# Moving half of the attention output projection out of the last head into a stage of its own

## The reference

```python
kqv = layernorm(x) @ Wqkv + bqkv                 # k, q, v in this order
scores = einsum('bsnh,btnh->bnst', k, q) / sqrt(128)   # masked, softmax
x = x + attn_out @ Wo + bo                       # Wo is 2048 x 2048
g = layernorm(x) @ Wg.T;  u = layernorm(x) @ Wu.T      # dequantized from uint8
x = x + (silu(g) * u) @ Wd.T                     # 8192 inner columns
```

## Time and profile before

| | us |
|---|---|
| median of 3 runs | 3152.21 |
| the profiled execution | 3151.75 |
| its span, first to last instruction, slowest core | 3150.1 |
| spans of the eight cores | 3135.9 to 3150.1 |
| TensorE matmul busy in the span | 2486.1 |
| VectorE busy | 990.5 |
| ScalarE busy | 789.9 |

### The profile page before, as it was taken

How to read it: one execution, slowest core, us unless ns; L and a number is a source line. 1 busy time by engine, 2 the same in 40 slices (tenths; PEclk the granted TensorE clock), 3 DMA queues, 4 the chain that set the end, 5 groups by cost and what they waited for, 6 DMA issues and landing times.

```text
span 3150.1 us, 31073 instructions; the slowest of 8 cores (3135.9 to 3150.1 us)
## 1 busy us (share of the span) xinstructions
PE 2486.1 (79%) x12388; PEld 1158.7 (37%) x12624; DVE 990.5 (31%) x1236; ACT 789.9 (25%) x1076; POOL 26.2 (1%) x49
## 2 busy tenths in 40 slices
PE   1256777777777777745554799999999999999998
PEld 0123333334433333311222344444444444444443
DVE  0354333333333333312334323222222223232322
ACT  0233333333333333300100230303131221313030
POOL 0000000000000000000000000000000000000000
PEclk9977999999999999955577899999999999999999
DMA  7744111111111111030033110101010111101012
GB/s 98 145 144 108 21 21 21 21 21 31 31 21 21 21 21 21 1 120 27 14 102 106 56 51 21 51 21 51 20 51 31 44 37 39 43 31 51 20 41 107
DMA packets 26573, 149.46 MB, mean 47 GB/s; under 512 B 2400, under 2 KB 2448, under 8 KB 19008
## 3 DMA queue, kind: packets, MB, share of 16 engines
q0 software_dynamic: 6848, 55.19, 8.8%
q1 hardware_dynamic: 18720, 86.51, 8.2%
q10 hardware_dynamic: 864, 5.77, 0.5%
HBM read 173.15 MB, written 16.78 MB: 60 GB/s over the span
## 4 chain that ended last, share of the span: by engine, by line
PE 69%; DVE 12%; ACT 7%; issue 6%; DMA 3%; another core or an unknown queue 2%; DVEq 0%; ACTq 0%; POOL 0%; POOLq 0%; SPq 0%
PE PB L183 35%; PE PJP L183 16%; PE SC L183 12%; DVE STAT L183 6%; PE TP L183 3%; PE OP L183 3%; DVE YS L183 3%; ACT VF L183 1%; ACT PT L183 1%; ACT PS L183 1%; ACT PTB L183 1%; DVE PS L183 1%; DVE SC L183 1%; DMA YS<-x_q 1%
## 5 line engine op out<-in xcount | busy, mean ns | idle before, releaser
L183 PE MATMUL PJP<-XHF,WQKVB 128*128 128x512 bf16 x1967 | 481.1, 394 | 25.5 <-ACT KS L183 15.8
L183 PE MATMUL PB<-YF,GD 128*128 128x512 bf16 x2008 | 454.6, 382 | 23.1 <-DVE YS L183 18.3
L183 PE MATMUL PB<-YF,UD 128*128 128x512 bf16 x2007 | 450.0, 379 | 2.2
L183 PEld LDWEIGHTS PJP<-XHF,WQKVB 128*128 128x128 bf16 x2048 | 206.1, 101 | 278.9 <-issue 70.3
L183 PEld LDWEIGHTS PB<-YF,GD 128*128 128x128 bf16 x2048 | 200.9, 98 | 267.7 <-issue 30.5
L183 DVE SCALAR_TENSOR_TENSOR HBUF<-PB,USC,SIG 128x1024 bf16<-128x1024 f32 x64 | 82.2, 1284 | 681.9 <-PE PB L183 681.9
L183 PEld LDWEIGHTS PB<-YF,UD 128*128 128x128 bf16 x2048 | 200.4, 98 | 241.6
L183 ACT ACTIVATE SIG<-PB,GSC 128x1024 f32<-128x1024 f32 x64 | 71.3, 1114 | 739.4 <-PE PB L183 739.4
L183 PE MATMUL SC<-DDG,HBUF 128*128 128x512 bf16 x1003 | 224.6, 379 | 13.7 <-DVE HBUF L183 12.6
L183 PE MATMUL PB<-DDG,HBUF 128*128 128x512 bf16 x1003 | 224.8, 379 | 1.1
L183 PE MATMUL PJP<-WOC,OS 128*128 128x512 bf16 x249 | 115.0, 611 | 102.4 <-DVE YS L183 88.1
(11 more groups left out here) (71 smaller groups left out, 1724.5 us busy)
## 6 DMA issues: line engine op xcount, KB each, us to landing
GUD<-u_blob SPq DMA_DIRECT2D x62, 768.0 KB, 4.3
WQKVB<-f_blob POOLq DMA_DIRECT2D x16, 1536.0 KB, 12.4
XT<-x_full SPq DMA_DIRECT2D x16, 1024.0 KB, 6.1
WOC<-wo_bf SPq DMA_DIRECT2D x12, 1024.0 KB, 6.1
wo_bf<-f_blob POOLq DMA_DIRECT2D x1, 8192.0 KB, 97.3
XT<-x_q SPq DMA_DIRECT2D x8, 1024.0 KB, 5.9
WOC<-wo_bf POOLq DMA_DIRECT2D x8, 1024.0 KB, 6.0
out<-YS POOLq DMA_DIRECT2D x8, 1024.0 KB, 4.2
```

The costliest lines, as they stand in the source:

```text
L183: r = getattr(e, meth)(*args, **kw)
```

## The change

The 64 projection groups in the last head go, and with them the waits that stood for them. The output projection stage now takes all 16 contraction chunks c = 0 to 15 in each of its 8 bursts, so each WOC buffer is filled twice per burst. The first load of WOC0 now waits for the last product of the head (attn_last), as that of WOC1 does already. The 8 loads of x into YS are all issued by POOL, each behind the one before; they are emitted after the head in the program, but POOL has nothing between. At the end the stores of odd row tiles are issued by ScalarE and not by POOL.

```diff
-            if h == HEADS - 1:
-                for _ in range(8):
-                    if tw_state["idx"] < len(tail_groups):
-                        emit_tail_wo()
             emit_tav()
...
+    ev_xq = []
+    p.wait("gpsimd", xhf_rel)
...
+    for j in range(QT):
+        if j:
+            p.wait("gpsimd", ev_xq[-1])
+        ev_xq.append(p.op("gpsimd", "dma_start",
+                          out=YS[:, j * 2048:(j + 1) * 2048],
+                          in_=xq_hbm[j * 128:(j + 1) * 128, :], inc="sxq",
+                          dma=True))
...
-    woc_rel = [[tw_state["last_mm"]], [attn_last]]
+    woc_rel = [[attn_last], [attn_last]]
...
-            for c in range(8, NCH):
+            for c in range(NCH):
...
-                            start=(c == 8), stop=last_c,
+                            start=(c == 0), stop=last_c,
...
-                p.wait("vector", [ev_wo_j[jl], ev_xq[j]]
-                       + tail_ev.get((j, dh), []))
+                p.wait("vector", [ev_wo_j[jl], ev_xq[j]])
...
-    ev_out = None
+    ev_out = [None, None]
     for j in range(QT):
-        p.wait("gpsimd", final_evac[j])
...
+        qeng = "gpsimd" if j % 2 == 0 else "scalar"
+        p.wait(qeng, final_evac[j])
...
+                             inc=SO if j % 2 == 0 else "so2", dma=True)
```

More of the change, by code:

```diff
@@ L593, in build_nc @@
     tp_rel_tp = tp_rel
[L594 to L634, removed]
     for h in range(HEADS):
@@ L758, in build_nc @@
                 p.wait("tensor", ev_woc)
-                if c == 8:
+                if c == 0:
                     p.wait("tensor", [os_done, pj_rel[0], pj_rel[1]])
@@ L932, in build_nc @@
             hbuf_rel[cc2] = ev_dn_last
-    ev_out = None
+    ev_out = [None, None]
     for j in range(QT):
-        p.wait("gpsimd", final_evac[j])
[L937 to L940, removed]
+        qeng = "gpsimd" if j % 2 == 0 else "scalar"
+        p.wait(qeng, final_evac[j])
+        ev_out[j % 2] = p.op(qeng, "dma_start",
+                             out=out_hbm[j * 128:(j + 1) * 128, :],
+                             in_=YS[:, j * 2048:(j + 1) * 2048],
+                             inc=SO if j % 2 == 0 else "so2", dma=True)
+    p.wait("gpsimd", ev_out[0])
+    p.wait("gpsimd", ev_out[1])
     p.build()
```

## The result

| | before | after |
|---|---|---|
| median of 10 runs each, us | 3152.75 | 3060.38 |
| the same without the runs with a lowered clock, us | 3151.35 | 3057.08 |
| ratio, 95% interval | | 0.9702 [0.969, 0.9714] |
| the profiled execution, us | 3151.75 | 3056.95 |
| its span, us (spans of the eight cores) | 3150.1 | 3055.4 (3045.5 to 3055.4) |

Forecast were 3057 us and a range of 3033 to 3092. In some executions, of either kernel, the cores of one half of the chip are granted a lower clock and take some per cent longer; such runs raise the first row of the table and are left out of every ratio and of every median that follows. The second row is 94.3 us apart, and the ratio gives 93.9.

A forecast was written before the change was run, and what follows sets the result against it. The last head's 64 small projection groups were taken as a chain of TensorE-VectorE round trips. Head, first burst, seven bursts and rest: 62.4 + 30.0 + 140.0 + 103.3 = 335.7 for 429.6; with stores -0.5, 3057 us, range 3033 to 3092.

The forecast's parts named there:

- The head: Last attention head, first score matmul to last copy: only its own chain stays, 62.4 us for 250.0, bounds 58 to 67.
- What is gained: Last head and projection stage: same number of matmuls, the gain is 64 small round trips between TensorE and VectorE.
- The loads of x: Eight chained loads on POOL during the last head: 54 us, hidden; nothing taken, 6 us kept for the range.
- The first burst: Start of the projection stage, no chunk loaded: ends 30.0 us after the head, 12.9 more, bounds 25 and 36.
- The seven bursts: Later projection bursts of 64 matmuls with load waits: 20.0 us each, 140.0 in place of 59.2.
- The rest of the stage: Projection stage outside the bursts, VectorE's adding, bias and layer norm with TensorE waiting: 103.3 us, unchanged.
- The stores: Final stores, odd row tiles issued by ScalarE: -0.5 us, between -1 and +1.
- The sum: Last head plus projection stage: 335.7 us for 429.6, -93.9; with the stores 3057 us in all.
- Loads in a crowd: Rival, projection bursts: eight cores' loads take 8.0 us instead of 6.0, +16, 3073 us; chance 0.12.
- Cold bursts: Rival, projection bursts: waits inside keep the clock at half, 27.7 us per burst, 3119 us; chance 0.10.
- Warm bursts: Rival, projection bursts: more matmuls make the cold start vanish, 17.5 us per burst, 3038 us; chance 0.05.
- Slower: Rival, projection stage: chunk loads become the bound, slower than before from 17.8 us landing, 3169 us at 20; chance 0.03.

The follow-up runs named there:

- four buffers: The changed kernel with two more Wo buffers, filled beside the last head, so that a burst has all four chunks; ratio 0.9577, median 3016.99 us.
- late weight loads: The changed kernel with ScalarE's two 768 KB GUD loads issued behind the first pair of row tiles, not at the head's end; ratio 0.9692, median 3050.97 us.

## Why the prediction was right, point by point

- **The head.** 62.4 us forecast, 62.36 measured (six cores 62.4, two 60.9). The chain of the attention alone could be read from the pieces between the groups. That it fits to a tenth is chance; the bounds were 58 and 67. The head is a chain of short operations on three engines: TensorE is busy for 28.1 of the 62.4 us, at a clock of 0.56.
- **What is gained.** The prediction closes its sum with "what is gained is the 64 small round trips". That is half of it. The number of matmuls is the same, but TensorE's busy time in head and stage falls from 226.0 us (140.09 + 85.88) to 181.2 (28.11 + 19.27 + 133.83): 44.8 of the 89.6 us that the traces show are the same matmuls taking less time, for the most part at a faster clock. The sum had this inside its measured terms (8.46 us for 32 matmuls in a burst, 14.9 for 32 in the small groups), without saying so.
- **The loads of x.** 54 us and hidden, forecast. They are issued from 1338.40 to 1377.95, one every 5.6 us and not 6.8, 45 us in all, and the last is in before the head ends. The stall of 24.4 us that went with them was worth 17 to 20 by itself.
- **The first burst.** 30.0 forecast, 36.3 measured, just outside the bounds of 25 and 36; the other seven cores have 33.2 to 35.5. This is the term that was mis-sized. "I take 11 for WOC0, near the middle" was one step: with four loads in flight the first matmul came 13.6 us after the head; without the GUD loads it came after 7.2. That is 2.6 of the 6.3 us. The other 3.7 are in "8.5 + 7.0 + 3.5": from the first matmul on 22.7 us passed and not 19.0 (18.4 to 22.7 on the eight cores, median 20.4), at a clock of 0.74. The first 32 matmuls took 9.61 us and not 8.46, and from their end 13.1 us passed and not 10.5, the last 32 taking 9.91 behind a wait of 3.43. The 8.46 were those of bursts that TensorE enters after some 5 us of standing. The runs show that this matters, though not in a strict order: 32 matmuls took 7.07 us after 0.52 us of idle time and 8.64 after 8.42 (four buffers), 9.44 after 7.6 (late weight loads) and 9.61 after 14.
- **The seven bursts.** 140.0 forecast, 137.65 measured, 19.66 each (130.5 to 138.2 on the eight cores). The windows of the longest and the shortest, and the sum of all seven:

```profile
1509.56:1531.41 21.85, 17.34 (x64) 6.81 (x64) 0.00 (x0) 0.00 (x0) 0.75 (x1) 0.84 0.49 156
...
1639.22:1657.55 18.33, 15.66 (x64) 6.45 (x64) 0.01 (x1) 0.00 (x0) 0.75 (x1) 0.91 0.38 124
sum 137.65, PE 114.79 PEld 46.49 DVE 0.51 ACT 1.75 POOL 5.24; mean PE 16.40 PEld 6.64 DVE 0.07 ACT 0.25 POOL 0.75
```

  Four take 18.3 to 18.8 us at a clock of 0.90 or 0.91, three 20.8 to 21.9 at 0.81 to 0.85. In these three the clock fell at a wait for part of the next matmuls: 16 took 5.30 us and not 3.61, behind 1.98 and 2.51 us, or 32 took 8.75 behind 4.07. The 1.0 us added for this was about right. Step by step in the burst shown above: 8.8 for the first 32 (8.46 forecast), 6.3 to the fourth chunk (7.0), 3.4 for its matmuls (3.5).
- **The rest of the stage.** 340.0 - 62.36 - 36.28 - 137.65 = 103.7 us, where 103.3 were forecast.
- **The stores.** Forecast -0.5; the traces show -0.15 and the runs nothing.
- **The sum.** 340.0 for 335.7 forecast, 4.3 too much. The profiled execution still came out at 3056.95 for 3057, because its head began at 1340.1 and not at 1345.5. Both are matters of the core that is read. Core 3 has the longest stage of the eight (268.3 to 277.6 us), and core 6 of the kernel before entered its head late (1337.1 to 1346.4, median 1342.3; after the change 1336.3 to 1343.1, median 1340.0). That 4.3 and 5.3 us cancel is luck. That the forecast holds is not: by the medians of the eight cores head and stage fall from 427.9 to 335.0 us, 92.9 for the 93.9 forecast, and the runs give 94.
- **The rivals.** Loads in a crowd: true of the first burst alone; the median landing of all WOC loads is 5.8 us, not 8. Cold bursts: no, bursts with a load wait in their middle run at 0.81 to 0.91. The Trainium skill, "TensorE: Matmul & The Clock Gate", section "Loop structure matters more than you think", expects a group behind a long wait for a transfer to run cold (8 us in its example). The trace agrees for the first burst: behind 14 us of waiting its first 32 matmuls took 9.61 us, and not 7.07. The waits inside the later bursts are shorter, and it shows there only in part: behind some waits of 2 us 16 matmuls took 5.30 us, behind others 3.61, the full clock. Warm bursts: no, 19.66 us and not 17.5, though four buffers, without waits, give 15.3 us for 64 matmuls at 0.89. Slower: the longest landing was 13.6 us on this core and 15.0 on any, under the 17.8 at which it decides.

## What to carry to other kernels

Filler work that hands every few matmuls to another engine and waits for the answer isn't filler: find its period in the timeline, multiply it by the number of groups, and compare it with the time of the chain that it is meant to fill. If such work has to stay, make its groups longer before anything else: eight matmuls took the time of four where the clock rose, and the edit gave 76 of the 94 us. And after a move, look for where transfers now start together: here six microseconds went to two loads whose data the kernel first needed at the end of the stage.

## What the runs showed of the hardware that I had not expected

- Groups of 4 matmuls with 0.94 us between kept a mean of 0.54 over 250 us, and 0.50 within the eight groups of a row tile (1507.24 to 1526.89). Groups of 8 with the same 0.94 us reached 0.76 in the mean of the head, and 0.90 from 1370 to 1400. A row of 32 that began 0.52 us after the head, whose own clock is about 0.56, took 7.07 us, the time at full clock.
- One load of 1024 KB landed in 5.1 to 6 us as a rule. When SP and POOL each started one at the head's end (late weight loads), SP's landed in 5.4 to 7.5 us and POOL's in 7.5 to 9.6 on the eight cores; with two of 768 KB beside them (changed kernel) it was 13.2 to 15.0 and 12.2 to 14.1.
